# Expert tiles of a decoder layer: the order of the last norm, the gathers and the scatters on VectorE, GpSimd and SyncE

## The reference

```python
x = _layernorm(x + attn(x, w_q, w_k, w_v, w_o))
x = _layernorm(x + xattn(x, ctx, Wq, bq, Wk, bk, Wv, bv))
# experts
gate = softmax(xf @ gate_w + gate_b)
topv, topi = top_k(gate, 2); topv = topv / topv.sum(-1)
for each expert e:
    h = relu(xf @ w1[e] + b1[e]);  y = h @ w2[e] + b2[e]
    out += y * combine[:, e]       # 0 for tokens that don't use e
x = _layernorm(x + out)
```

## Time and profile before

| | |
|---|---|
| runs | 1458.38 us median of 3 (1458.04 to 1459.02) |
| the profiled execution | 1459.59 us, span 1457.3 us, mean granted TensorE clock 0.989 |
| busy share of the span | PE 97%, DVE 74%, ACT 59%, POOL 38% |
| expert tiles | from about 888 us to the end |

### The profile page before, as it was taken

The page is one execution under the profiler, slowest core; times in us unless marked ns, Lnnn a source line. Parts: engine busy times, 40 slices in busy tenths (PEclk is TensorE's granted clock), DMA queues, the critical chain, the costliest instruction groups (busy, mean ns, idle before and its releaser), DMA issues.

```text
span 1457.3 us, 48882 instructions
## 1 busy us (share of the span) xinstructions
PE 1409.0 (97%) x18586; PEld 928.0 (64%) x18586; DVE 1080.8 (74%) x1970; ACT 861.4 (59%) x1966; POOL 556.7 (38%) x952
## 2 busy tenths in 40 slices
PE   7999999999999999999999899999999999999995
PEld 3344445444444544544444448888889999999994
DVE  6778788888888889888999974777655555555553
ACT  3477788877787777777878784333323333333331
POOL 1211121212212214412215212577776555555554
PEclk9799999999999999999999999999999999999998
DMA  5335455544434323422243323222432222222221
GB/s 161 96 95 155 125 166 159 151 115 130 112 103 130 114 63 114 112 70 67 73 137 107 77 84 143 69 78 88 129 96 77 78 74 74 74 74 74 74 76 52
DMA packets 108031, 147.44 MB, mean 101 GB/s; under 512 B 27258, under 2 KB 79786, under 8 KB 106778
## 3 DMA queue, kind: packets, MB, share of 16 engines
q1 hardware_dynamic: 93658, 105.71, 25.4%
q0 software_dynamic: 14000, 38.11, 7.9%
q10 hardware_dynamic: 144, 0.52, 0.1%
HBM read 81.09 MB, written 63.17 MB: 99 GB/s over the span
## 4 chain that ended last, share of the span: by engine, by line
PE 77%; DVE 10%; issue 5%; POOL 3%; DMA 2%; SPq 1%; ACT 1%; DVEq 0%; POOLq 0%; ACTq 0%
PE pa L912 14%; PE pa L1136 13%; PE pb L912 13%; PE pb L1150 13%; PE po L1083 13%; PE px L912 7%; DVE neg L1420 4%; PE px L905 2%; PE po L1012 1%; ACT w_sb L1239 1%; PE px L987 1%; POOL x_by_expert L787 1%; PE px L961 1%; SPq L476 1%; DMA space<-y_parts,y_tags 1%
## 5 line engine op out<-in xcount | busy, mean ns | idle before, releaser
L1420 DVE TENSOR_REDUCE neg<-pa 128x1 f32<-128x1024 f32 x512 | 612.3, 1214 | 84.6 <-PE pa L912 77.9
L1239 ACT ACTIVATE w_sb<-pb 128x512 f32<-128x512 f32 x996 | 590.2, 599 | 136.0 <-PE pb L912 101.2
L912 PE MATMUL pb<-w_sb 99*32 99x512 bf16 x3984 | 393.2, 381 | 4.2 <-ACT w_sb L1239 1.9
L1355 ACT ACTIVATE space<-pa,b1T_sb 128x128 f32<-128x128 f32 x568 | 154.7, 383 | 322.5 <-PE pa L1136 322.5
L912 PE MATMUL pa<-w_sb 96*32 96x512 bf16 (+1 forms) x4208 | 328.3, 385 | 11.5 <-DVE neg L1420 10.6
L1083 PE MATMUL po<-w_sb,space 128*32 128x256 f32 x4000 | 304.6, 379 | 0.0
L1136 PE MATMUL pa<-xgT,attn_t 128*128 128x128 f32 x2272 | 269.1, 275 | 1.1 <-DVE attn_t L1733 1.0
L1136 PEld LDWEIGHTS pa<-xgT,attn_t 128*128 128x128 f32 x2272 | 265.9, 192 | 6.6 <-issue 3.2
L1150 PE MATMUL pb<-w_sb,space 128*128 x1136 | 260.3, 379 | 0.0
L1150 PEld LDWEIGHTS pb<-w_sb,space 128*128 128x128 f32 x1136 | 208.8, 190 | 25.0 <-issue 0.3
L912 PEld LDWEIGHTS pa<-w_sb 96*32 96x32 bf16 (+1 forms) x4208 | 102.3, 97 | 136.0 <-DVE neg L1420 38.8
(11 more groups left out here) (236 smaller groups left out, 1228.4 us busy)
## 6 DMA issues: line engine op xcount, KB each, us to landing
y_parts<-attn_t SPq DMA_DIRECT2D x13, 896.0 KB, 5.4
w_sb<-w SPq DMA_DIRECT2D x17, 512.0 KB, 5.6
attention_out<-space SPq DMA_DIRECT2D x64, 128.0 KB, 1.8
w_sb<-w SPq DMA_DIRECT2D x7, 1024.0 KB, 8.0
xg<-x_by_expert SPq DMA_DIRECT2D x54, 130.0 KB, 2.2
q_parts<-w_sb SPq DMA_DIRECT2D x48, 128.0 KB
w_sb<-q_parts SPq DMA_DIRECT2D x64, 96.0 KB, 3.5
w_sb<-k_parts SPq DMA_DIRECT2D x64, 96.0 KB, 3.5
```

Of the source, the lines that this page charges most:

```text
L912: mm = pe.matmul(out[at:end], lhsT[:, at:end], rhs, start=start, stop=stop, tile_position=(0, at))
L1239: act.activation(ex_of(n)[:, half * HALF:(half + 1) * HALF], score_bank(n, half), ACT.Exp, scale=SCALE).then_inc(e_done, 1)
L1355: ins = act.activation(hT[tile % 2][:, f, :], pH[tile % 2][:, f, :], ACT.Relu, bias=g.b1_sb[:, bass.ds(e * FT + f, 1)])
L1420: dve.tensor_reduce(neg[i % 2][:, t:t + 1], pa[n % 2][:, :], AX.X, ALU.max, negate=True).then_inc(max_done, 1)
```

## The change

In the loops over the expert tiles, a new `token_tile` is true in tiles 2 to 10.

- VectorE: in all other tiles (1 and 11 to 70), `residual(t-1)` and `measure_3(t-1)` come ahead of `copy_w1(t+2, 0)`, and `norm_3(t-1)` stands between the two copies. In token tiles the order is as before: residual and measure_3 after both copies, norm_3 at the end of the step.
- GpSimd: in all other tiles `spread_3(t-1)` and `scatter_out(t-1)` come ahead of `gather(t)`. The gather comes ahead of the rows' scatters in all tiles. In token tiles spread_3 and scatter_out follow the rows' scatters, after the gather.
- `scatter(FFN_TILES - 1)`, the write of the last tile's result to `y_parts`, which nothing reads, is dropped.
- The last wait for `out_rows` moves from GpSimd's end to SyncE's end.

```diff
 @block.sync, at its end
+                sp.wait_ge(out_rows, 16 * FFN_TILES)

 @block.gpsimd, loop over tiles
                     if tile:
                         scatter(tile - 1)
...
+                    token_tile = MAIN_PROJ < j <= NT
+                    if tile and not token_tile:
+                        spread_3(tile - 1)
+                        scatter_out(tile - 1)
+                    if tile == 0:
+                        pool.wait_ge(zeros_in, 16 * ZEROS)
+                        pool.wait_ge(pv_done, PAIRS)
+                    gather(tile)
                     if 2 <= since < 6:
                         scatter_first(B - 2, 2 * (since - 2))
...
-                    if tile:
+                    if tile and token_tile:
                         spread_3(tile - 1)
-                    if tile == 0:
-                        pool.wait_ge(zeros_in, 16 * ZEROS)
-                        pool.wait_ge(pv_done, PAIRS)
-                    gather(tile)
-                    if tile:
                         scatter_out(tile - 1)
-                scatter(FFN_TILES - 1)
                 spread_3(FFN_TILES - 1)
                 scatter_out(FFN_TILES - 1)
-                pool.wait_ge(out_rows, 16 * FFN_TILES)

 @block.vector, loop over tiles
+                    token_tile = MAIN_PROJ < j <= NT
+                    if tile and not token_tile:
+                        residual(tile - 1)
+                        measure_3(tile - 1)
                     if tile + 2 < FFN_TILES:
                         copy_w1(tile + 2, 0, e)
                     if MAIN_PROJ < j < NT:
                         norm_1(j)
+                    if tile and not token_tile:
+                        norm_3(tile - 1)
...
                     if tile + 2 < FFN_TILES:
                         copy_w1(tile + 2, 1, e)
-                    if tile:
+                    if tile and token_tile:
                         residual(tile - 1)
                         measure_3(tile - 1)
...
-                    if tile:
+                    if tile and token_tile:
                         norm_3(tile - 1)
```

## The result

The changed kernel takes 1557.54 us in the median of 6 runs (1554.78 to 1559.02); the kernel before took 1458.56 beside it (6 runs, 1456.96 to 1460.42). The ratio is 1.068, with a 95% interval of 1.0669 to 1.0691. The direction and the mechanism of the forecast held; its size was 12.5 us short.

What follows compares the result with a forecast made beforehand. TensorE was taken to bound the kernel at 7.245 us a tile; the change closes a loop of seven terms summing to 8.67 us. 59 turns, plus token tiles and end, gave 1545.0 us, 5.9% slower, range 1514 to 1580.

Steps and rivals of the forecast that it cites:

- The bound and the loop's length: Tiles 11 to 70: a closed loop from gather to gather takes 8.67 us against TensorE's 7.245 us a tile.
- The term of the copy: Loop step from L1817's end to norm_3, with a w1 copy beside spread_3: 1.34 us, lower bound 0.96.
- scatter_out beside the copy: Loop step scatter_out: 1.05 us if the w1 copy ends before it, 1.29 if the copy runs beside it.
- Part 3: Tiles 11 to 19, rows' scatters behind the gather: 0 to 0.36 us in 8 tiles, +1 us in all.
- Part 2: Token tiles 2 to 10, gather ahead of rows' scatters and spread_3: +4 us, bounds 0 and +8.
- Part 4: Kernel's end: dropping scatter(70) gains nothing, moving the last wait to SyncE gains 1.5 us, or 0.
- The rival by which the gain would be 0: Kernel's end: GpSimd waits for its own transfers anyway, so moving the last wait gains 0; no chance given.
- The sum: Whole kernel: gather(11) at 1018.7, gather(70) at 1530.4, span 1543.9, profiled run 1546.2, median 1545.0 us.
- The loop under TensorE's period: Rival, steady tiles: loop stays below 7.245 us, so about 1457 to 1461 us, or 1455 to 1456; chance 0.06.
- the overlap of its parts: Rival, steady tiles: GpSimd prepares scatter_out during its wait, spread_3 undisturbed; 7.7 to 8.2 a turn, 1488 to 1517 us; chance 0.06.
- The loop of 9.73 us: Rival, steady tiles: landings of 3.7 us in all turns and the copy delaying scatter_out, 1608 us; chance 0.08 for above 1580.
- The clock: Way to be wrong: TensorE's granted clock falls with new idle time until its 7.245 us of work passes 8.67.

Runs made afterwards that it cites:

- e1: Changed kernel with gather(t) moved back between spread_3(t-1) and scatter_out(t-1) on GpSimd in tiles 11 to 70: 1500.78 us, ratio 1.0007 to the kernel before.
- e5: Changed kernel with one spare 128x1 power on GpSimd between scatter_out and gather in tiles 1 and 11 to 70: 1614.50 us, ratio 1.0771.
- e6: Kernel before with one spare 128x1 power on GpSimd between spread_3 and gather in tiles 1 and 11 to 70: 1459.94 us, ratio 1.0007.
- e10: Changed kernel with norm_3 right behind measure_3, ahead of both copies of w1: 1569.20 us, ratio 1.0476 to the kernel before.
- a2: The changed kernel itself measured a second time, nothing altered: 1587.89 us, ratio 1.0595 to the kernel before.
- e2: Changed kernel with VectorE's order of before the change; GpSimd's and SyncE's new order stay: 1577.24 us, ratio 1.051 to the kernel before.
- e8: Kernel before with VectorE's new order and the two end edits, GpSimd's order otherwise as before: 1469.74 us, ratio 1.0068.
- e3: Kernel before with only the end edits, last scatter dropped and last wait moved from GpSimd to SyncE: 1456.12 us, ratio 0.9981.
- e4: Kernel before with the gather ahead of the rows' scatters and spread_3 in token tiles 2 to 10 only: 1465.71 us, ratio 1.0041.
- e7: Kernel before with four spare 128x1 powers on GpSimd between spread_3 and gather in tiles 1 and 11 to 70: 1570.99 us, ratio 1.0468.
- e11: Kernel before with VectorE's new order, both end edits, and spread_3 and gather ahead of rows' scatters in tiles 1 and 11 to 70: 1499.54 us, ratio 1.0008.

## Why the prediction was right, point by point

**The bound and the loop's length: right.** "8.67 us a tile against 7.245." The median turn from gather(20) to gather(70) is 8.69 us, and the seven terms in the turn shown above measured 2.84, 1.74, 1.38, 0.41, 0.92, 1.04, 0.31 against 2.90, 1.74, 1.34, 0.41, 0.93, 1.05, 0.30: each is within 0.06. Between 1100 and 1540 us there are 51 gathers, and the residual waited for one 50 times, where it had been nine times (waits of VectorE's L1808: us, times, longest):

```profile
DVE space L1808 <- DMA space<-y_parts,y_tags: 166.5, 50, 5.0
```

e1 shows the cause by undoing it alone, e5 and e6 that a loop's time counts in the one kernel and not in the other.

**The term of the copy: right in size, wrong in place.** I took 1.34 from a row in which the power is stretched to 0.88, and said that spread_3's power, L845, would be at 0.8 to 0.9. It stayed at 0.57; the addition ahead of it, L844, went from 0.19 to 0.60, since the copy starts 0.13 ahead of it and not between the two. The term is 1.38 all the same, and that the two come so close is luck: the row that I took it from has another overlap. e10 gives its price when that copy is elsewhere.

**scatter_out beside the copy: right.** 1.05 was taken and 1.29 kept as a bound; the mean is 1.048, as the copy is over by 0.3 us when scatter_out starts (1414.93 + 0.68 against 1415.93). e10, where copies run beside it, has 1.18. The Trainium skill, page "SBUF — State Buffer", section "SBUF: two separate sides", says that VectorE and GpSimd share a way to SBUF that one of them holds at a time; the two fences of e10 and of the changed kernel agree with it in kind, as the copy lengthens whichever of GpSimd's instructions it meets. In the changed kernel's steady turns the addition ends 0.04 to 0.05 us behind the copy every time, as if it had stood until then. What the copy lengthens an instruction by, 0.41 us at an addition and 0.13 at a scatter, only the runs tell. The last is less than the whole remainder of the copy that I had derived for a scatter behind it: the copy reaches 0.28 us into the scatter in e10.

**The turns on average: too short.** The mean of those 50 turns is 8.777 (438.84 us in all), not 8.67, which makes +5.3 us, or +6.1 with the 0.8 that I took off for the last two. Term by term, the 6.1 us are 2.1 in the gap ahead of the gather, 2.0 in the wait for spread_3 (1.38 a turn and not 1.34), 1.3 ahead of scatter_out and only 0.6 in the landings, since I had taken 2.90 for these where the median is 2.87. Eight turns are longer than 9 us, and they are of three kinds.

In one GpSimd stood 2.04 us with nothing in the trace to wait for:

```profile
1427.78 1.04 POOL L838 DMA_INDIRECT space<-y_parts,y_tags  x1 [2.04 <-issue]
```

In two, those that begin with gather(36) and gather(43), scatter_out started 1.50 to 1.52 us behind norm_3 instead of 0.93. In the other five, from gathers 26, 35, 44, 53 and 62, the residual started 3.21 to 3.46 us behind the gather, in all the others 3.06 at most. Most of this comes back in other runs. In a2 GpSimd stands 2.05 us ahead of the same gather(57), in e2 and e10 2.05 and 1.90, and the same two scatter_outs are late in all three. The five late landings have a companion: the trace lists transfers of the kind "instruction", of 16 KB, on DMA queue 8, and one starts 0.9 to 1.2 us behind the gather in just these five turns. One of them, in the view of the DMA queues from 1232.2 to 1235.6:

```profile
q8 instruction: 1, 0.02, 1.6%
```

In a2 one starts 1.1 to 1.8 us behind the gather in the turns from gathers 26, 35, 53, 62 and 64, and the residual starts 3.49 us or more behind the gather in these and 3.16 at most in all others. The two go together; no experiment moved such a transfer, so that it delays the gather is likely and not shown. In a closed loop each such wait is paid for, so the total goes by the mean, while a sum from medians of rows gives the median turn.

**Part 3, the rows' scatters behind the gather: the step that failed.** I said +1 us in all for tiles 11 to 19. gather(11) to gather(20) took 83.2 us against 71.3 in the kernel before and 9 x 8.67 + 1 = 79.0 forecast: 5.2 over the bare loop, not 1. The loop's terms divide it. 2.5 us lie between measure_3 and norm_3. Half of that is one turn, gather(16)'s, in which the reweight stands ahead of the scatters; I named it and gave it no price of its own. The scatters' end and norm_3 in that turn:

```profile
1069.21 1.07 POOL L860 DMA_INDIRECT y_parts<-space,y_tags  x1 [0.30 <-issue]
1070.30 0.20 POOL L844 TENSOR_TENSOR c_all<-c_all,neg_half 128x1 f32<-128x1 f32 x1
...
1071.18 0.41 DVE L1824 TENSOR_SCALAR space<-space,c_all 128x256 f32<-128x256 f32 x1 [1.75 <-POOL c_all L846]
```

norm_3 comes 2.58 us behind the sums there instead of 1.34. In the turns from gathers 14, 15, 18 and 19 the same step takes 1.58 to 1.64, so for plain scatters the estimate of 0 to 0.36 each was right. Another 2.3 us lie between gather and residual, for which I had added nothing: in the turns from gathers 11 and 12 VectorE itself comes to the residual 3.46 and 3.33 us behind the gather, busy with other work, and in those from 13 and 17 it is 4.06 and 3.31, with a landing as what it waited for. 0.3 us is a late scatter_out. I had compared GpSimd's time for three scatters (5.0) with the time of the sums (4.64) and looked no further. e8 loses 13.6 us without the closed loop (1469.74 against the 1456.12 of e3), in the same tiles, through copies of w1 that come late; that part is only half explained, as said above.

**Part 2, the token tiles: right in size.** The stretch from the transposes (L1012, L1014 after) of tile 3 to those of tile 11 went from 86.55 to 91.29 us: +4.7 against +4; gather(11) itself came 3.1 later. Alone, in e4, the stretch is 93.16, +6.6. The 1.9 us between the two lie in tiles 8 and 9. In the changed kernel's profile the scatter into y_parts had landed when the gather of step 8 came up, and it stood 0.18 us; norm_3 then waited 2.21. In e4 the gather stood 1.54 and norm_3 3.67, and in a2, the changed kernel again, 1.70 and 3.68. That this wait can move in front of spread_3 I had left out, and whether it does differs between runs of one kernel.

**Part 4, the end: right.** Behind the last scatter_out there are 4.99 us in the changed kernel and 5.2 in e3, against 6.89 before: 1.7 to 1.9 gained where 1.5 was taken. That scatter's end in the changed kernel:

```profile
1546.66 1.05 POOL L854 DMA_INDIRECT out<-space,y_tags  x1 [1.38 <-DVE space L1824]
```

The rival by which the gain would be 0 (GpSimd waits for its own transfers anyway) is out. That both end edits together gain this is shown, not how it divides between them.

**The sum, again against the profiled run** (1554.78, span 1552.7; forecast 1546.2): gather(11) at 1017.87 instead of 1018.7, -0.8; part 3's tiles +4.2 beyond the forecast; the 50 turns behind them +6.1; then gather(70) to the end of scatter_out 7.77 instead of 8.0, -0.3; the rest -0.4; outside the span -0.2: 8.6, as the profiled runs have it. The remaining 4 us are of another kind: I took the median as 1.2 below the profiled run, as it was in the kernel before, and this time the profiled run was the fastest of six and the median 2.8 above it. One profiled run's place among the runs is chance and can't be carried over.

**The rivals.** The loop under TensorE's period and the overlap of its parts are out by the terms; e6 shows that the former is right for a loop that has the room. The loop of 9.73 us is out as a mean, but single turns came near it. The clock, which I named as a way to be wrong, fell in two places and lengthened no turn; the one of 10.49 us came before the fall, not behind it.

**What stays open.** At the level of 1499 us the change costs 89 us and not 99 (ratio 1.0595 against 1.068), though its steady turns are as long there (mean 8.84). e7, whose code is that of the kernel before but for the powers, reaches the transposes of tile 11 at 1035.83 there, 27 us later than the kernel before did at the lower level (1008.82). The other 13 us between the levels must come later, and e1 and e11 have turns of up to 11.5 us in tiles 12 to 20. So it may be that the kernel before is bound by something else in these tiles and has less to lose; it was not profiled at that level, so this is argued, not shown. Open too are what makes the level, the 2.04 us of GpSimd, what the instruction transfers do to a gather, and the cause of the rest of e8's loss.

## What to carry to other kernels

Before an instruction is moved in an in-order queue, write down the circle through it (what it waits for, who waits for it, what is queued behind either) and compare its length with the period of the engine that bounds the kernel: under the period half a microsecond is free (e6), above it nearly every fraction is paid in each tile (e5, e7). Sum a closed loop with mean durations, rare waits included, and read the terms in the order that the change makes, since a copy stretches what it then runs beside. Ask too by which way the loop reaches the bounding engine: here the copies of w1 in one order and the loads of rows in another (e2). Ramps deserve their own circle: the same order of VectorE cost nothing in the steady part and 13.6 us through nine tiles in which GpSimd had other work (e8).

## What the runs showed of the hardware

- An addition of 128x1 on GpSimd takes 0.19 us alone and 0.59 to 0.61 when a VectorE copy of 128x1024 starts just ahead of it; in the changed kernel's steady turns it ends 0.04 to 0.05 us behind the copy. A gather of 128 rows takes 1.09 alone, and 1.53 in the mean of e7, where it runs beside copies.
- From the end of norm_3 to the start of the indirect DMA that waits for it GpSimd took 0.92 to 0.94 us in all but three of the 50 steady turns of the changed kernel, and 1.22 to 1.52 in these; between two queued ones it is 0.30. The wait itself has a price of 0.6 us, which a reordering can put into a loop or take out of it.
- A gather in flight while an instruction transfer of 16 KB starts on DMA queue 8, 0.9 to 1.2 us behind it, reached its reader after 3.21 to 3.46 us, all others of those turns after 3.06 at most. That is seen in five turns, not tested.
- The span ends about 5 us after GpSimd's last indirect DMA where SyncE holds the last wait (4.99 in the changed kernel, 5.2 in e3), and 6.9 us after it where GpSimd does.
- The same kernel before takes 1459 or 1499 us, 2.8% apart, in different groups of runs, more than most of the parts here are worth.
